# An audio tower on one core: opening loads, table load and dummy products rearranged, and a maximum over partitions moved from POOL to PE and VectorE

## The reference, cut to what matters

```
h = patches(x) @ W + b                                   # 64 x 45 x 128
h = h + attn(layernorm(h))                               # Nystrom attention
h = h + ffn(layernorm(h))                                # 8 experts, the 2 best, softmax weights

attn(x): q, k, v = layernorm(x)*gamma+beta, padded in front to 64 rows, @ w_qkv; 8 heads of 16
         attn1 = softmax(q k_l^T); attn2 = softmax(q_l k_l^T); attn3 = softmax(q_l k^T)
         out = attn1 @ (pinv(attn2) @ (attn3 @ v)) + conv33(v);  x + out @ w_out + b_out

pinv(a): denom = max(rowsum |a|) * max(colsum |a|)       # both maxima over ALL batch elements and heads
         z = a^T / denom
         6 times: z = 0.25 z (13 I - a z (15 I - a z (7 I - a z)))
```

## Time and profile before

| what | value |
|---|---|
| median of 3 runs | 633.38 us (631.23 to 635.68) |
| profiled execution, its own time | 632.56 us |
| its span | 630.8 us |
| PE busy | 580.2 us (92% of the span) |
| ACT, DVE busy | 385.6 us (61%), 383.3 us (61%) |
| POOL busy | 311.6 us (49%) |

### The profile page before, as it was taken

The page is one execution under the profiler, slowest core; times in us unless marked ns, Lnnn a source line. Parts: engine busy times, 40 slices in busy tenths (PEclk is TensorE's granted clock), DMA queues, the critical chain, the costliest instruction groups (busy, mean ns, idle before and its releaser), DMA issues. The chain is left out here.

```text
span 630.8 us, 40775 instructions
## 1 busy us (share of the span) xinstructions
PE 580.2 (92%) x17503; PEld 476.8 (76%) x17503; DVE 383.3 (61%) x1096; ACT 385.6 (61%) x783; POOL 311.6 (49%) x450
## 2 busy tenths in 40 slices
PE   1899999998899899999999999999999999989996
PEld 1587777776467788887887887887887887867774
DVE  4446666664256367588588588588588588343332
ACT  1357666676558348568668668668668668244442
POOL 2767677763167455555655655655655654100000
PEclk9979999999889799999999999999999999999999
DMA  2500000100000011011011011111011011000000
GB/s 61 146 18 11 9 8 12 28 2 2 3 3 1 21 36 42 25 35 40 26 34 53 25 37 44 32 38 38 25 50 38 25 41 38 3 13 0 13 13 13
DMA packets 26264, 17.40 MB, mean 28 GB/s; under 512 B 3020, under 2 KB 25700, under 8 KB 26212
## 3 DMA queue, kind: packets, MB, share of 16 engines
q1 hardware_dynamic: 24388, 14.11, 7.8%
q0 software_dynamic: 672, 2.12, 1.2%
q10 hardware_dynamic: 1152, 0.53, 0.3%
HBM read 15.27 MB, written 1.48 MB: 27 GB/s over the span
## 5 line engine op out<-in xcount | busy, mean ns | idle before, releaser
L458 POOL TENSOR_TENSOR T<-Q,W 128x368 f32<-128x368 f32 x192 | 182.4, 967 | 162.7 <-issue 145.4
L606 ACT ACTIVATE Q<-P 64x368 f32<-64x368 f32 x384 | 195.3, 508 | 89.0 <-DVE P L816 80.2
L948 PEld LDWEIGHTS bank<-P 46*46 46x46 f32 x6144 | 155.1, 122 | 34.1 <-issue 26.3
L948 PE MATMUL bank<-P 46*46 46x46 f32 x6144 | 168.9, 208 | 7.6 <-DVE P L816 3.2
L948 PE MATMUL bank<-W 46*46 46x46 f32 x6144 | 166.7, 208 | 0.0
L948 PEld LDWEIGHTS bank<-W 46*46 46x46 f32 x6144 | 151.1, 121 | 0.1
L806 DVE SCALAR_TENSOR_TENSOR W<-Q,bank 128x368 f32<-128x368 f32 x192 | 101.9, 531 | 27.1 <-PE bank L948 20.0
L816 DVE SCALAR_TENSOR_TENSOR P<-T,bank 128x368 f32<-128x368 f32 x160 | 85.1, 532 | 35.1 <-PE bank L948 32.6
L642 ACT ACTIVATE hT<-bank,b_sb 128x360 f32<-128x360 f32 x128 | 69.7, 559 | 54.5 <-PE bank L948 52.0
L948 PE MATMUL bank<-xnT,w1c 128*128 x168 | 61.9, 491 | 11.3 <-issue 11.3
L914 DVE SCALAR_TENSOR_TENSOR acc<-bank,wt,acc 120x128 f32<-120x128 f32 x144 | 41.6, 344 | 47.3 <-PE bank L948 47.3
(11 more groups left out here) (133 smaller groups left out, 766.7 us busy)
## 6 DMA issues: line engine op xcount, KB each, us to landing
w2c<-in_L_ffn_w SPq DMA_DIRECT2D x42, 128.0 KB
w1c<-in_L_ffn_w SPq DMA_DIRECT2D x42, 128.0 KB, 2.0
w_sb<-in_L_ffn_w POOLq DMA_DIRECT2D x2, 1024.0 KB, 7.4
pat<-in_x SPq DMA_DIRECT2D x24, 60.0 KB
out<-outb SPq DMA_DIRECT2D x24, 60.0 KB
wqkv_sb<-in_L_attn_w_qkv ACTq DMA_DIRECT2D x1, 192.0 KB, 2.7
band<-scratch SPq DMA_DIRECT2D x2, 66.1 KB
cn<-in_consts ACTq DMA_DIRECT2D x1, 72.0 KB, 1.8
```

The costliest lines, as they stand in the source:

```text
L458: pool.tensor_tensor(out=T[g], in0=Q[g], in1=W[g], op=ALU.add).then_inc(s_t[g], 1)
L606: ins = act.activation(Q[g][to, :, :], P[g][fro, :, :], ACT.Copy, scale=T_IN)
L948: return pe.matmul(out, lhsT, rhs, start=start, stop=stop, skip_group_check=True)
```

## The change

Opening: gam and bet move from ACT's queue to SP's, between the patches of block 0 and kraw. tokw and tokb get a semaphore of their own, `s_tw`. A small activation (from normT into lamc, whose value is later overwritten) stands after the issue of wqkv on ACT's queue and is then ACT's first activation. PE waits for the patches alone before the transposes, for `s_tw` before the embedding, and for the rest (`s_wa`: gam, bet, wqkv, bout) after it; ACT and POOL wait for `s_wa` one piece later than before, DVE only for `s_tw`. DVE clears the banks in another order, and PE waits for three of them first. Four dummy products of 128x128 stand before the transposes, six of 128x384 (`keep_warm`) between the embedding and the transposes of the norm.

Seam: POOL's reduction goes. PE multiplies each column of `den` with the identity, which gives a row of 128 numbers on partition 0 of a PSUM bank; DVE takes the maximum of both rows in one instruction, multiplies, and takes the reciprocal on one partition; PE spreads it to 128 partitions by a product with a row that holds RHO, and DVE copies that column into lamc. The five dummy products become six, divided 1, 2, 3 around these products.

```diff
-WARM_A, WARM_B, WARM_C = 1, 5, 1
+WARM_A, WARM_C, WARM_P, WARM_Q = 1, 1, 4, 6
+WARM_B = (1, 2, 3)
...
-        N_WA, N_WC = 6, 6
+        N_TW, N_WA, N_WC = 2, 4, 6
...
             load_patches(0)
+            sp.dma_start(gam_sb[:, :], gamma.unsqueeze(1)).then_inc(s_wa, 16)
+            sp.dma_start(bet_sb[:, :], beta.unsqueeze(1)).then_inc(s_wa, 16)
             sp.dma_start(kraw[:, :], res_k.rearrange("h a k b -> h (a k b)")).then_inc(s_kraw, 16)
             load_patches(1)
...
             pool.wait_ge(s_init, N_INIT)
+            roots(0)
             pool.wait_ge(s_wa, 16 * N_WA)
-            roots(0)
             residual(0)
...
-            pool.wait_ge(s_den, 2)
-            pool.partition_all_reduce(den2[:, :], den[:, :], 128, RMAX).then_inc(s_den2, 1)
...
             act.dma_start(cn[:, :], consts).then_inc(s_cn, 16)
-            act.dma_start(tokw_sb[:, :], tok_w).then_inc(s_wa, 16)
-            act.dma_start(tokb_sb[:, :], tok_b.partition_broadcast(128)).then_inc(s_wa, 16)
-            act.dma_start(gam_sb[:, :], gamma.unsqueeze(1)).then_inc(s_wa, 16)
-            act.dma_start(bet_sb[:, :], beta.unsqueeze(1)).then_inc(s_wa, 16)
+            act.dma_start(tokw_sb[:, :], tok_w).then_inc(s_tw, 16)
+            act.dma_start(tokb_sb[:, :], tok_b.partition_broadcast(128)).then_inc(s_tw, 16)
             act.dma_start(wqkv_sb[:, :], w_qkv).then_inc(s_wa, 16)
+            act.wait_ge(s_init, 1)
+            act.activation(lamc[:, :], normT[:, 0, 0:1], ACT.Copy)
             act.dma_start(bout_sb[:, :], b_out.partition_broadcast(128)).then_inc(s_wa, 16)
             act.dma_start(wout_sb[:, :], w_out).then_inc(s_wb, 16)
...
-            act.wait_ge(s_wa, 16 * N_WA)
             act.wait_ge(s_init, N_FIRST)
             patches(0)
+            act.wait_ge(s_wa, 16 * N_WA)
             normed(0)
...
-            for bk in bank:
+            for bk in [bank[n] for n in (3, 0, 2, 1, 4, 5, 6, 7)]:
                 dve.memset(bk[:, :], 0.0).then_inc(s_psum, 1)
...
-            dve.wait_ge(s_wa, 16 * N_WA)
+            dve.wait_ge(s_tw, 16 * N_TW)
+            dve.memset(rho_row[:, :], RHO).then_inc(s_m2, 1)
...
             dve.wait_ge(s_den2, 1)
-            dve.tensor_tensor(out=dprod[:, :], in0=den2[:, 0:1], in1=den2[:, 1:2], op=ALU.mult).then_inc(s_dmax, 1)
+            dve.reduce_max(m2[:, :], bank[4][0:1, 0:256].rearrange("p (c n) -> p c n", c=2), AX.X).then_inc(s_dmax, 1)
             dve.wait_ge(s_dmax, 2)
-            dve.reciprocal(drec[:, :], dprod[:, :]).then_inc(s_dmax, 1)
+            dve.tensor_tensor(out=dprod[:, :], in0=m2[:, 0:1], in1=m2[:, 1:2], op=ALU.mult).then_inc(s_dmax, 1)
             dve.wait_ge(s_dmax, 3)
-            dve.tensor_scalar(lamc[:, :], drec[:, :], RHO, None, ALU.mult).then_inc(s_lamc, 1)
+            dve.reciprocal(drec[:, :], dprod[:, :]).then_inc(s_m2, 1)
+            dve.wait_ge(s_den2, 2)
+            dve.tensor_copy(lamc[:, :], bank[4][:, 256:257]).then_inc(s_lamc, 1)
...
-            pe.wait_ge(s_psum, 8)
+            pe.wait_ge(s_psum, 3)
             pe.wait_ge(s_init, N_FIRST)
             pe.wait_ge(s_cn, 16)
...
+            for _ in range(WARM_P):
+                mm(bank[3][:, 0:128], ident, ident)
+            patches(0)
+            pe.wait_ge(s_tw, 16 * N_TW)
+            embed(0)
+            pe.wait_ge(s_psum, 8)
             pe.wait_ge(s_wa, 16 * N_WA)
-            patches(0)
-            embed(0)
+            for _ in range(WARM_Q):
+                keep_warm()
             normed(0)
             qkv(0)
...
-            for _ in range(WARM_B):
-                mm(bank[5][:, :], ident, w1_sb[:, 0:2, :].rearrange("p e f -> p (e f)"))
+            def bridge(n):
+                for _ in range(n):
+                    mm(bank[5][:, :], ident, w1_sb[:, 0:2, :].rearrange("p e f -> p (e f)"))
+
+            bridge(WARM_B[0])
+            pe.wait_ge(s_den, 2)
+            mm(bank[4][0:1, 0:128], den[:, 0:1], ident)
+            mm(bank[4][0:1, 128:256], den[:, 1:2], ident).then_inc(s_den2, 1)
+            bridge(WARM_B[1])
+            pe.wait_ge(s_m2, 2)
+            mm(bank[4][:, 256:257], rho_row[:, :], drec[:, :]).then_inc(s_den2, 1)
+            bridge(WARM_B[2])
```

More of the change, by code:

```diff
@@ L39 @@
 AX = mybir.AxisListType
-RMAX = bass.bass_isa.ReduceOp.max
 B, L, C = 64, 375, 8
@@ L196, in tower @@
         den = sb("den", [128, 2])
-        den2 = sb("den2", [128, 2])
-        dprod = sb("dprod", [128, 1])
-        drec = sb("drec", [128, 1])
+        m2 = sb("m2", [1, 2])
+        rho_row = sb("rho_row", [1, 128])
+        dprod = sb("dprod", [1, 1])
+        drec = sb("drec", [1, 1])
         lamc = sb("lamc", [128, 1])
@@ L233, in tower @@
         outb = sb("outb", [TT, TILES, D])
+        s_tw, s_m2 = sem("s_tw"), sem("s_m2")
         s_cn, s_wa, s_wb, s_wc = sem("s_cn"), sem("s_wa"), sem("s_wb"), sem("s_wc")
```

## The result

The changed kernel took 627.93 us (median of 8 runs, 626.01 to 631.04) against 632.34 (629.58 to 635.68) for the kernel before: ratio 0.993, 95% interval 0.990 to 0.9959. Over all runs of this study it is 627.68 on average (31 runs) against 632.38 (81 runs): 4.7 us; one run of the changed kernel, 632.79 and over 1.5% above its fastest, is left out of its mean. Direction and range held; of the 7.8, 4.4 to 4.7 came, a little over half. The profiled execution of the changed kernel took 626.01, span 624.2.

The account below looks back on a forecast made before the run. PE, busy 92% of the span, was taken as the bound, waiting on chains of short steps at opening and seam. 632.56 less 3.95 (opening) less 3.85 (seam) gave 624.8 us, the sum's range 622 to 628, overall 619.5 to 629.5.

Parts of the forecast that it names:

- Opening, 3.95 forecast: Opening: split waits, early table load and dummies start the first scaled tile X 3.95 sooner, bounds 3.1 to 4.7.
- POOL's issues as the next thing late: Opening: X could start at 22.1 by DVE, but POOL's last weight load issue ends only at 22.7.
- Rival 1: First block: its half-speed spell, 4.24 lost, may shorten or vanish, giving down to 620.6; chance 0.20.
- Seam, 3.85 forecast: Seam: lamc 2.6 sooner, next iteration's Q at 168.5 in place of 172.36; 3.85 gained, bounds 1.0 to 4.9.
- PE does not idle, so I take no fall of the clock: Seam: PE works through its bridge products without a gap, so squares take 1.15, not 2.31, and dummies 0.9, not 2.00.
- two bridge products (1.8): Seam: two dummy products keep PE until 161.6, ahead of the product that spreads the reciprocal; lamc at 162.0.
- the prediction's own sign of being wrong: Seam: the forecast is wrong if the detour replacing POOL's reduction lasts over 4.
- The rest of the term: Behind lamc: squares 1.15 in place of 2.31, dummies 0.9 in place of 2.00, T following W without the 2.3 wait.
- The page rule on partition reductions: Seam: assigns reductions along partitions to GPSIMD, not VectorE; by it the seam gains nothing, time 628.6.
- Rivals 2, 3 and 4: 2: opening dummies stay half speed, 629.4, chance 0.15; 3: seam gives little, 0.10; 4: more half-speed spells, 636, 0.05.
- Rival 3: Seam gives 0 to 1.0, as the detour takes 5.36 or the clock falls; 627.6 to 628.6, chance 0.10.
- Theory D: Formed after the first experiments: seam worth lamc's gain, 2.1 at full speed, next to nothing at half; the rest is slack.

Follow-up runs that it names:

- last_block_filled: The changed kernel with three more dummy products of 128x384 in PE's gaps in the last block of the first half; 624.96 us, ratio 0.9882 to the kernel before.
- after_again: The changed kernel, no edit, timed again in the first set of experiments; 627.27 us, ratio 0.9917 to the kernel before.
- after_third: The changed kernel, no edit, timed again as the measure of the third set; 626.71 us, ratio 0.9926 to the kernel before.
- before_again: The kernel before, no edit, timed again in the first set; 632.85 us, ratio 1.0012 to the kernel before.
- reduce_aside: The changed kernel with POOL's reduction over partitions made all the same, into a tile nobody reads; 628.35 us, ratio 0.993 to the kernel before.
- the pair above: Traces of the changed kernel with the old seam (627.08 us, ratio 0.991 to the kernel before) and of the changed kernel itself, compared from lamc to the seventh P.

## Why the prediction held its direction and lost half its size

*Opening, 3.95 forecast.* At X the traces with the new opening and its dummies as they are have 22.6 to 23.1 (mean 22.92 of eight), those with the old one 26.65, 27.09, 27.18 (26.97): 4.05 (`last_block_filled`, whose last block differs, is left out here and below). The parts were right too: transposes at 6.68 (6.4 forecast), bias addition 9.94 (9.6), kraw 7.81 (7.9), dummies' end 15.65 (15.0), and POOL's issues as the next thing late, level with DVE in the first trace and up to 0.9 behind it in others. What was missed is that the gain grows on the way: den's last instruction starts at 153.94 (mean of the eight) against 159.89, 5.95 sooner. Spells in the first half differ: that of block 0 takes some 3.5 us in five of the eight and some 10 in three; with the old opening 7 to 10. Rival 1 came true by half, in some runs.

How long that spell lasts goes with a moment in the opening, the one at which the dummies speed up. Timeline and a window of `after_again`:

```profile
9.35 5.08 PE L952 MATMUL bank<-wqkv_sb,cn 128*128 128x384 f32 x12
```
```profile
25.00:35.50 10.50, 10.50 (x137) 8.09 (x133) 5.47 (x14) 4.17 (x10) 8.47 (x16) 0.51 0.43 117
```

Here the twelve take 5.08, in the first trace 6.12. In the five traces with a short spell they take 5.90 to 6.21, the spell begins between 30.1 and 31.1, and den comes between 152.9 and 153.7. In the three with a long one they take 4.99 to 5.56, it begins between 25.1 and 26.4, and den comes between 154.7 and 155.5. `after_third`, at 6.21, has the spells of the first trace in the same places (30.9, 201.6 and 621.4 for 31.0, 201.6 and 621.5). So an early rise went with the later den, and the kernel sets only when the dummies begin, not when they speed up. Why one brings the other is not shown. The Trainium skill, TensorE: Matmul & The Clock Gate, Part 1, says that the moment of the rise shifts from run to run of one kernel. The traces agree: it came after three to six of the twelve.

*Seam, 3.85 forecast.* The step that failed is "PE does not idle, so I take no fall of the clock", with "two bridge products (1.8)" in front of the product that spreads the reciprocal. It was right for what follows the bridge and wrong for the bridge itself: the spell had begun before. In the traces with 1, 2, 3, lamc comes 3.8 after den where PE is granted full speed (four) and 5.4 to 5.7 where half (three), against 5.8 to 5.95 by POOL, in whose three traces PE was granted full speed at the seam twice and half once (`before_again`, 5.79). So 2.6 became 2.1 or 0.1 to 0.5, and in the three traces the prediction's own sign of being wrong showed, a detour of over 4. The rest of the term, some 1.25 from squares at full speed and a T on time, was seen as forecast at the first P and was given back by the seventh: slack, shown by `reduce_aside` and by the pair above. The page rule on partition reductions (the Trainium skill, GPSIMD Engine Reference, 4.1 Engine selection) thus comes out about even at half speed, 5.4 to 5.7 against 5.8 to 5.95, and loses at full speed, 3.8. In the time of the whole kernel what it stood for came true: the new seam alone gained nothing, 0.9992.

*Rivals 2, 3 and 4.* The six dummies did speed up, after three to six of the twelve instructions, where I had four. Rival 3, given 0.10, is what came at the seam: it gave little, and 627.93 lies in that rival's 627.6 to 628.6. Its second reason, the clock, is the one that the traces show; but the rival had it slow the squares behind the bridge, and it slowed the bridge. More half-speed time was not seen: 23.6 us per run before, 22.1 after.

*The sum.* By its own runs the opening gives 5.0 (medians) to 5.7 (ratio), the seam 0 to 0.5, where 3.95 and 3.85 were forecast; 4.4 to 4.7 came, the parts and the whole agreeing within the intervals. Two errors of opposite sign left the time inside the range, which is luck in part. The range that the prediction gives the sum alone, 622 to 628, should by its own bounds have been 623.0 to 628.5 (632.56 less 4.7 and 4.9, less 3.1 and 1.0).

What stays open: why spells sit over the seam in some runs (the gaps of the last block are likely, not shown); why block 0's spell goes with the moment of the rise; and why a seam that is 2.1 sooner in four of seven traces gains nothing in the run times, though a lamc that is sooner still does. Theory D fits the traces, but the times don't bear out its 2.1.

## What to carry to other kernels

A dummy product that keeps PE's clock up also stands in PE's queue: put the products of the critical chain ahead of it, and price the dummy at half speed, since it is in a half-speed spell that it lasts longest (2.08 us against 1.13 here). When a step behind the seam arrives sooner, follow it for some iterations before crediting it: here slack had swallowed it by the seventh P. And one profiled execution shows one throw of the clock: a gain read from spells that a trace happens to hold is not a gain.

## What the runs showed of the hardware

- After the reduction over partitions POOL's next instruction starts 2.2 to 2.6 after its input, with or without a reader of the result (0.2 without the reduction).
- ACT's queue issued bout at 3.27, though the table load from 3.21 to 4.49 and the small activation at 4.50 stand ahead of it in the program: the issue did not wait for either, where the prediction had it wait.
- The column of the granted clock shows 1.00 all through the opening, where the projections took 2.82 without the dummies and 1.50 with them: before the first fall of a trace the durations alone tell the speed.
- Early in the second half PE stops for about 2.1 us with no releaser (before: 210.1 to 212.2; changed: 200.1 to 202.1, with a transfer on the queue for instructions just ahead), and a half-speed spell of 7 and of 14 us begins within 2 us of the stop's end. Nothing was tried against it.
